# A mixture-of-experts step loop regrouped into two-step cycles, with its indirect DMAs in bursts

## What is computed

```python
# first half: x = x + layernorm(four S4D layers of layernorm(x))
z = _layernorm(x)                      # 8192 tokens x 128 channels
gating = z @ router_w.T                # 8 experts
probs = softmax(gating)
topk_weights, selected_experts = top_k(probs, 2)
for e in range(8):
    ew = sum(topk_weights * (selected_experts == e))
    h = z @ w1[e].T                    # 128 -> 512
    y = h[:, 256:] * silu(h[:, :256]) @ w2[e].T   # 256 -> 128
    out = out + y * ew
x = x + _layernorm(out)
```

## Time and profile before

| | us |
|---|---|
| median of the 3 runs (1073.33 to 1079.39) | 1076.9 |
| span of the profiled execution | 1076.0 |
| first silu of the expert loop starts | 700.9 |
| last second product starts | 1015.9 |
| PE, DVE, ACT, POOL busy, share of the span | 67%, 71%, 51%, 48% |

### The profile page before, as it was taken

How to read it: one execution, slowest core, us unless ns; L and a number is a source line. 1 busy time by engine, 2 the same in 40 slices (tenths; PEclk the granted TensorE clock), 3 DMA queues, 4 the chain that set the end, 5 groups by cost and what they waited for, 6 DMA issues and landing times.

```text
span 1076.0 us, 25371 instructions
## 1 busy us (share of the span) xinstructions
PE 724.1 (67%) x8523; PEld 611.2 (57%) x8524; DVE 761.7 (71%) x1889; ACT 551.7 (51%) x1197; POOL 521.3 (48%) x704
## 2 busy tenths in 40 slices
PE   0039267794879948795878876677877787787600
PEld 0028267673866658673876655565766676676500
DVE  8978867587675966588675998456555565565697
ACT  7628940188104941079103877333555574565645
POOL 2113224165432654257342766655676626536385
PEclk9999679797988979798988985578999999999955
DMA  7807699963999279982995002211343444444224
GB/s 283 349 1 223 210 385 386 331 243 122 358 340 380 74 258 385 329 299 65 359 386 227 1 11 79 68 36 52 108 125 122 124 120 119 124 117 121 86 82 151
DMA packets 120745, 205.48 MB, mean 191 GB/s; under 512 B 18381, under 2 KB 43481, under 8 KB 119769
## 3 DMA queue, kind: packets, MB, share of 16 engines
q1 hardware_dynamic: 112984, 188.66, 49.5%
q0 software_dynamic: 7680, 15.74, 5.4%
HBM read 167.40 MB, written 36.96 MB: 190 GB/s over the span
## 4 chain that ended last, share of the span: by engine, by line
issue 31%; PE 23%; POOL 20%; DVE 11%; ACT 8%; another core or an unknown queue 2%; DMA 2%; POOLq 1%; SPq 0%; ACTq 0%; DVEq 0%
PE bank L1197 10%; POOL zbuf L614 6%; POOL rstd_of L603 5%; PE bank L1216 4%; POOL toep L696 3%; PE bank L1032 3%; PE bank L1010 2%; ACT glu_work L969 2%; DVE glu_work L1797 1%; POOL sums L594 1%; DMA toep<-kernels_dram 1%; ACT toep L906 1%; ACT glu_work L949 1%; ACT ln_tmp L895 1%
## 5 line engine op out<-in xcount | busy, mean ns | idle before, releaser
L1032 PE MATMUL bank<-zbuf,toep 128*128 128x128 f16 (+3 forms) x3328 | 146.0, 206 | 90.1 <-DVE zbuf L1412 72.2
L1197 PE MATMUL bank<-toep 128*128 128x256 f16 x1248 | 162.2, 283 | 57.0 <-issue 31.0
L1032 PEld LDWEIGHTS bank<-zbuf,toep 128*128 128x128 f16 x3328 | 142.5, 102 | 94.2 <-issue 48.5
L1197 PEld LDWEIGHTS bank<-toep 128*128 (+1 forms) x1248 | 118.3, 101 | 90.5 <-issue 70.2
L614 POOL TENSOR_TENSOR zbuf<-zbuf,w_cur 128x256 f32<-128x256 f32 x120 | 89.7, 749 | 143.0 <-DVE zbuf L1476 142.9
L680 POOL DMA_INDIRECT z_sorted<-toep x120 | 124.2, 1035 | 68.3 <-remote 25.3
L1476 DVE TENSOR_REDUCE zbuf<-bank 128x256 f32<-128x512 f32 x128 | 87.1, 688 | 71.3 <-PE bank L1032 71.2
L1067 PE MATMUL bank<-wo_cur,glu_work 128*128 128x256 f32 x512 | 134.2, 407 | 2.5 <-ACT glu_work L840 2.2
L840 ACT ACTIVATE glu_work<-bank,unscale_cur 128x512 f32<-128x512 f32 x64 | 42.8, 668 | 167.4 <-PE bank L1054 167.3
L1067 PEld LDWEIGHTS bank<-wo_cur,glu_work 128*128 128x128 f32 x512 | 96.3, 198 | 43.4 <-issue 17.8
L1767 DVE SCALAR_TENSOR_TENSOR toep<-bank,toep 128x256 f16<-128x256 f32 x88 | 37.3, 424 | 93.5 <-issue 74.8
(11 more groups left out here) (269 smaller groups left out, 1488.8 us busy)
## 6 DMA issues: line engine op xcount, KB each, us to landing
toep<-kernels_dram SPq DMA_DIRECT2D x104, 1024.0 KB, 14.0
glu_work<-kernels_dram SPq DMA_DIRECT2D x16, 1024.0 KB, 14.1
toep<-z_sorted SPq DMA_DIRECT2D x88, 128.0 KB
y_sorted<-toep SPq DMA_DIRECT2D x88, 128.0 KB
z_sorted<-ln_tmp SPq DMA_DIRECT2D x3, 3072.0 KB, 23.8
toep_last<-kernels_dram SPq DMA_DIRECT2D x8, 1024.0 KB, 14.1
hres<-in_x SPq DMA_DIRECT2D x1, 4096.0 KB, 13.0
toep<-in_x SPq DMA_DIRECT2D x1, 4096.0 KB, 23.9
```

The source lines that it names most:

```text
L1032: last = MM(dst[:, d * (B // 4):, :], toep_slot(g)[:, c, d * P:(d + 1) * P, k], z_conv[:, 0:QUADS - d * (B // 4), g * GROUP + c].rearrange ...
L1197: last = MM(out[:, piece % 2 * XP:(piece % 2 + 1) * XP], w1_row[:, pw, bass.ds(e + piece * P, P)], xT_s[:, px * XP:(px + 1) * XP], start=( ...
```

## The change

It reorders the expert loop and changes how the tokens are divided. Nothing in the S4D layers changes.

- Three quads are dense (3, 14 and 15) instead of one, and three lists are sorted (12, 20 and 20 tiles; 19 + 27 + 27 = 73 blocks) instead of four. That makes 73 + 48 = 121 steps instead of 104, and 104 scatters and 104 gathers instead of 120 and 120.
- The sorted steps come first, the dense ones last.
- The loop goes in cycles of two steps. In a cycle PE transposes the two blocks of two cycles ahead, does both second products of two cycles back, then both first products. ACT does both silus, one copy of double width (512) for the two inputs, both high halves, and one copy of double width for the two outputs. DVE goes likewise.
- POOL waits once per burst, for `s_hid` of both steps of a cycle, and then issues 4 (both lists' scatters), 3 (gathers of lists 0 and 1) or 2 (list 2) indirect DMAs.
- The input and output blocks keep four slots each, `xT` has four instead of two; SP stores 12 blocks behind the load instead of 7.
- The last `count` and `places`, which stood in the loop, and `leads` with its exponentials move ahead of the loop. The dense steps, which PE ran in a hardware loop, are written out; only sorted steps 8 to 67 are in one.
- At the end, five gathered pieces (12, 16, 4, 12, 8 tiles) come first and the three dense quads last.

```diff
-CHOICES = ((0, 12), (12, 20), (32, 16), (48, 16))
+CHOICES = ((0, 12), (12, 24), (36, 20), (56, 8))
-DENSE = (3,)
+DENSE = (3, 14, 15)
-SEGMENTS = ((0, 12), (16, 16), (32, 16), (48, 16))
+SEGMENTS = ((0, 12), (16, 20), (36, 20))
+    CHOOSE_AT.append(max([_q + 10] + PLACE_AT[-1:]))
+    PLACE_AT.append(CHOOSE_AT[-1] + 2)
-GATHERED = [(0, 12), (16, 16), (32, 16), (48, 8), (56, 4), (60, 2), (62, 2)]
-PIECES = [(4 * q, 4) for q in DENSE] + GATHERED
+GATHERED = [(0, 12), (16, 16), (32, 4), (36, 12), (48, 8)]
+PIECES = GATHERED + [(4 * q, 4) for q in DENSE]
+EARLY = 4
+LOOPED = 8
+TURNS = (EXPERT_TILES - 6 - LOOPED) // UNROLL + 1
+STEPS = EXPERT_TILES + DENSE_STEPS
+LATE = 4
+BURSTS = (4, 4, 3, 2)
+def cycles(eng, cycle):
+    for s in range(-EARLY, LOOPED, 2):
+        cycle(Step(s))
     with eng.Fori(0, TURNS) as i:
+        for s in range(LOOPED, LOOPED + UNROLL, 2):
+            cycle(Step(s, i))
+    for s in range(LAST_STEPS, STEPS + LATE, 2):
+        cycle(Step(s))
...
+            LAG = 12
+            for n in range(0, EXPERT_TILES + LAG + 1, 2):
+                for tile in (n, n + 1):
+                    if tile < EXPERT_TILES:
+                        load(tile)
+                for tile in (n - LAG, n - LAG + 1):
+                    if 0 <= tile < EXPERT_TILES:
+                        store(tile)
...
+            def in_burst(size, most):
+                if left[0] == 0:
+                    burst[0] += 1
+                    pool.wait_ge(s_hid, min(2 * burst[0], most))
+                    left[0] = size
+                left[0] -= 1
...
-                    in_step()
+                    if transfers[0] >= 36:
+                        in_burst(BURSTS[0] if g == 1 else BURSTS[1], (FIRSTS[g] - 6) // 2 * 2 + 2)
+                    elif transfers[0] % 3 == 0:
+                        pool.wait_ge(s_z2T, min(6 + transfers[0] // 3, QUADS))
+                    transfers[0] += 1
...
+                    burst[0] = max(burst[0], (FIRSTS[g] + XTS[g]) // 2 + 3)
...
+                        in_burst(BURSTS[3] if g == SEGS - 1 else BURSTS[2], STEPS)
...
+            def cycle(s):
+                steps = two(s, lambda t: t.is_step)
+                for t in steps:
+                    silu(t)
+                ahead = two(s + EARLY, lambda t: t.is_sorted)
+                if ahead:
+                    xT_high(ahead)
+                if steps and s.at >= LATE:
+                    act.wait_ge(s_yps, (s + (len(steps) - LATE)).n)
+                for t in steps:
+                    inner_high(t)
+                done = two(s + -LATE, lambda t: t.is_sorted)
+                if done:
+                    act.wait_ge(s_yps, (s + (2 - LATE)).n)
+                    y_out(done)
...
+            def cycle(s):
+                if s.is_sorted:
+                    pe.wait_ge(s_xTsb, s.pair + 1)
+                for t in two(s + EARLY, lambda t: t.is_sorted):
+                    transpose_in(t)
+                for t in two(s + -LATE, lambda t: t.is_step):
+                    second_product(t)
+                for t in two(s, lambda t: t.is_step):
+                    first_product(t)
...
             gates()
+            leads()
+            def cycle(s):
+                steps = two(s, lambda t: t.is_step)
+                for t in steps:
+                    gated(t)
+                ahead = two(s + EARLY, lambda t: t.is_sorted)
+                if ahead:
+                    xT_low(ahead)
+                for t in steps:
+                    inner_low(t)
+                for t in two(s + -LATE, lambda t: t.dense):
+                    accumulate(t)
```

More of the change, by code:

```diff
@@ L711, in _ @@
                 scatter(g)
-            for i in range(len(DENSE), len(PIECES)):
+            for i in range(len(GATHERED)):
                 if PIECES[i][0] == SEGMENTS[-1][0]:
@@ L1135, in _ @@
                     route(q - 10)
[L1136 to L1138 removed]
+                    for c in range(SEGS):
+                        if q == max(CHOOSE_AT[c] + 1, 14):
                             count(c)
@@ L1225, in _ @@
+            cycles(pe, cycle)
         @block.vector
@@ L1801, in _ @@
-            tile_steps(dve, step, False)
+            def cycle(s):
[9 more added lines that the diff above has]
+                    accumulate(t)
+            cycles(dve, cycle)
```

310 lines of the change are left out of this document (130 added, 180 removed).

## The result

The changed kernel takes 1082.3 us (median of 20 runs, 1077.7 to 1087.3) against 1079.3 for the kernel before in the same runs: ratio 1.003, 95% interval 1.002 to 1.005. I had forecast 1063 us, so the time is 19 us above the forecast, and the change gains nothing here: the kernel is 0.3% slower.

What follows compares the result with a forecast made beforehand. Waits hold the loop: POOL's DMAs cost PE 0.93 us a step. Terms: 702.2 + 105.4 + 2.6 + 7.6 + 101.2 + 4.4 + 76 + 2.0 + 4.5 + 56.5 = 1062.4 us, median 1063, range 1045 to 1086.

Steps and rivals of the forecast that it cites:

- Rows of three beside sorted cycles: Loop's gathers of lists 0 and 1: 22 bursts of 4.6 us each, 101.2 us, bounds 4.4 to 4.7 each.
- a cycle takes the longer of PE's work and POOL's period: Expert loop: PE's 4.4 us sorted or 3.96 dense against POOL's period per burst; the longer sets the cycle.
- 1.3 us after `s_hid`: Loop: next first product needs only silu 0.60 and gate product 0.69; PE has 0.4 + 1.5 us to do first.
- the free cycle: Loop, between the gather lists: one cycle without a burst, 4.4 us.
- Rows of four and block 19: Loop's scatters: 17 bursts of 6.2 us, 105.4 us; waiting for block 19's load makes one cycle 13.8, 7.6 us lost.
- The start: Ahead of the loop: first two hidden products end at 702.2 us, bounds 4 us either way.
- may cost 2 us or nothing: Routing stretch before 690: the `count` of 20 tiles stands two quads later, costing 2 us or nothing.
- The dense part: Loop's bursts of two: PE bounds, 19 cycles of 4.0 us, 76 us, bounds 3.8 to 4.4 each.
- the rival of late instructions: Written-out PE code: instructions arrive late, 2 us at each of 10 transfers, 1083 us; chance 0.16.
- The rival of the port: Loop bursts: DVE stretches POOL's DMAs to 1.3 us each, 1102 us; chance 0.05.
- The end: Behind the last hidden product: drain 4.5 us, then DVE's pieces to the end 56.5 us, bounds 53 to 59.

Runs made afterwards that it cites:

- two_edits: Changed kernel with eight more of list 1's scatters ahead of the loop and PE's sorted cycles written out: 1062.5 us, 0.990 of before.
- free group: Experiments run on one chip with the kernel before beside them, where that kernel takes 988 to 993 us.
- before_no_pool: Kernel before without its scatters from the 37th on and all but the first gather of each piece: 994.1 us, 0.927 of before.
- eight_more_before_loop: Changed kernel with eight more of list 1's scatters issued ahead of the loop without a wait for PE's steps: 1071.0 us, 0.991 of before.
- held: Said of groups of runs in which the kernel before takes 1075 to 1081 us; the runs of the result were such.
- no_pool_again: Changed kernel without the last 68 scatters and all but the first gather of each piece, second run: 1029.5 us, 0.954 of before.
- changed_once_more: Changed kernel, unaltered, as a control: 1041.1 us, 1.051 of before.
- group 3: Four experiments: before without transfers, before with rows of four, one row of 28, and two edits; before took 1075.1 us.
- group 4: Four experiments: PE written out again, the experts' register load moved again, and two kernels with rows of three; before took 989.3 us.
- row_of_28: Changed kernel with list 1's last 28 scatters in one row instead of seven rows of four: 1086.8 us, 1.011 of before.
- three_edits: Changed kernel with PE written out, counting behind the last quad's transposes and eight more scatters ahead of the loop: 1085.2 us, 1.004 of before.

## Why the prediction was wrong, step by step

**Rows of three beside sorted cycles (the largest term, +9.2 us).** The step that failed is "a cycle takes the longer of PE's work and POOL's period", with 4.6 us from a single interval of before, and under it the reason given: the first product needs only silu and gate product "1.3 us after `s_hid`". PE's own 4.40 us stands: two_edits shows it where POOL rests (transposes at 853.81 and 858.21). The same kernel shows what three transfers do to it, and the changed kernel shows one such cycle whole. First two_edits, then the changed kernel:

```profile
853.81 0.60 PE L1184 MATMUL bank<-ident,toep 128*128 128x128 f32 x4
...
858.21 0.60 PE L1184 MATMUL bank<-ident,toep 128*128 128x128 f32 x4
...
878.92 0.94 POOL L711 DMA_INDIRECT zbuf<-y_sorted,toep  x1 [1.17 <-PE bank L1212]
...
883.20 1.44 PE L1230 MATMUL bank<-toep,glu_work 128*128 x23 [0.40 <-issue]
...
883.74 0.94 POOL L711 DMA_INDIRECT zbuf<-y_sorted,toep  x1 [1.03 <-PE bank L1212]
...
884.83 2.79 PE L1212 MATMUL bank<-toep 128*128 128x256 f16 x24 [0.18 <-issue]
```

```profile
878.01 2.79 PE L1212 MATMUL bank<-toep 128*128 128x256 f16 x24 [0.22 <-issue]
...
881.48 1.08 ACT L958 ACTIVATE glu_work<-bank 128x512 f32<-128x512 f32 x2 [1.84 <-PE bank L1212]
...
882.20 1.29 DVE L1797 TENSOR_TENSOR glu_work<-bank,glu_work 128x512 f32<-128x512 f32 x2 [1.93 <-issue]
...
883.03 2.79 PE L1212 MATMUL bank<-toep 128*128 128x256 f16 x24 [0.24 <-issue]
886.70 0.65 PE L1184 MATMUL bank<-ident,toep 128*128 128x128 f32 x4 [0.87 <-issue]
```

In two_edits the rows came 4.82 us apart (878.92 to 883.74), and PE stopped for 0.17 to 0.40 us. The stop of 0.40 in the second product cost nothing by itself, for the first gate product was ready only at 884.69. The one ahead of the first products is marked "issue", but it is the wait for data, as beside rows of four. In the changed kernel the first products ended at 880.80 and both silus started only at 881.48, 1.00 us after the row before (880.49); the first gate product ended at 882.89 (0.69 us from 882.20), and the next first products started at 883.03, 0.14 us later. The cycle is 2.79 + 0.68 + 1.55 = 5.02 us. So the cycle is neither PE's 4.40 nor POOL's 4.6 but the sum along a closed chain: first products, a post that comes late beside the row, silu, gate product, first products. Unheld, this chain has 1.48 us to spare (above, free group). I had read the late post, and used it for POOL's period alone, not for ACT, which waits for the same semaphore.

Of the 9.2 us, 15 ordinary intervals between rows of three beside sorted cycles, 4.91 us in the mean for 4.6, make 4.7. Four beside the first dense cycles (4.72) make 0.5. Three long ones (5.44, 5.62 and 11.17 around the free cycle, for 9.0) make 4.0. At 883.03 above a turn of the loop follows: branch and register load stand behind the first products, and PE idled 0.87 us before the transposes. I had left that bubble at nothing. Before has a second product at that place, and its turns cost 0.13 us (cycles of 4.41 and 4.54 us by turns in before_no_pool).

**Rows of four and block 19 (+2.4).** 6.33 us (mean of 13) for 6.2, and 14.9 us (747.22 to 762.11) for 13.8; the first two rows came as one, unbroken, and took 13.9 us (708.05 to 721.96) for the 15.0 of the sum, which was luck. The wait was where I had put it, at the transposes of block 19:

```profile
755.44 0.69 PE L1184 MATMUL bank<-ident,toep 128*128 128x128 f32 x2 [10.39 <-DMA toep<-z_sorted]
```

Working out its price from POOL's last row was right; not asking what it would bring to start those scatters earlier was the omission, since POOL stood idle for 10.38 us just ahead of the loop. eight_more_before_loop did that and gained 10 us.

**The start (+5.8).** 3.5 us of it are no part of the change. PE's routing begins at 612.95 in the changed kernel's profiled execution and at 609.45 in that of before, in work that is the same in both, and over all profiled executions it began anywhere from 608 to 618 us:

```profile
612.95 0.28 PE L1132 MATMUL bank<-router_sb,toep 128*128 128x8 f32 x2
...
691.30 1.88 PE L1132 MATMUL bank<-router_sb,toep 128*128 128x8 f32 x8 [2.36 <-ACT toep L933]
```

Of the other 2.3 us, 2.05 lie between the first routing and the last (78.35 us here, 76.30 before), and they are again a late post. I had said of the counting, which now stands ahead of the last transposes, that it "may cost 2 us or nothing". It moved the transposes by 0.1 us (74.61 us after the first routing, 74.52 before). But the copy that waits for them started 1.22 us after their end, behind a row of POOL's that ended at 688.60, and in the kernel before 0.04 us after it. First the changed kernel, then before:

```profile
687.56 1.38 PE L1120 MATMUL bank<-ident,toep 128*128 128x128 f32 x4
690.16 0.60 ACT L929 ACTIVATE toep<-bank 128x512 f16<-128x512 f32 x1 [5.80 <-PE bank L1120]
```

```profile
683.97 1.09 PE L1090 MATMUL bank<-ident,toep 128*128 128x128 f32 x4
...
685.10 0.60 ACT L918 ACTIVATE toep<-bank 128x512 f32<-128x512 f32 x1 [1.38 <-issue]
```

Whether the post would have come in time without the counting ahead of it is not shown: that edit alone ran only in a free group.

**What held.** The dense part: PE's first products 3.98 and 4.09 us apart by turns beside rows of two (4.0 forecast), steps 72 to 120 in 98.4 us held and 96.6 free.

```profile
961.96 2.80 PE L1212 MATMUL bank<-toep 128*128 128x256 f16 x24
962.19 1.27 POOL L711 DMA_INDIRECT toep<-y_sorted,toep  x1 [0.30 <-issue]
965.94 2.80 PE L1212 MATMUL bank<-toep 128*128 128x256 f16 x24
```

This is written-out code at PE's full rate, so the rival of late instructions is refuted there; PE written out from end to end needed 75 transfers on q8 for 61 and was no slower (1.051 of before in either form, in free groups). The rule of the Trainium skill, "Runtime: NRT & Kernel Launch", section on instruction fetch mechanics, that sequential prefetch is mostly hidden, fits the trace: no stop in dense cycles. Its other half, that a branch can force a fetch, does not explain the 0.87 us at the turn above: from 757 to 890 us the changed kernel shows no instruction transfer on q8. The rival of the port had 0.3 us of truth: the second transfer of a dense row takes 1.27 us for 0.95. The rule of the Trainium skill, "SBUF — State Buffer", section on the two separate sides, that DVE in a two-port mode keeps GpSimd from writing descriptors, would allow for that, but no run here shows that DVE is the cause. DVE's pace with and without transfers is the same (dense cycles 3.97 and 4.09 in no_pool_again and in changed_once_more). The end was right to 0.6 us: 60.4 us from the last silu on, for 61.0.

**Behind the sum.** I had seen that the loop would take about as long for 17 more steps, and so staked the whole gain of 13.6 us on the end and on periods known to 0.2 us, 60 times over. An error of 0.3 us in a cycle is 18 us. The gain of the forecast was no larger than that error, and a single interval of three transfers was no ground for the term: it is the first behind 17 us in which POOL stood idle.

## What to carry to other kernels

Where an engine is slowed by another's transfers, price a cycle by the number beside it, each length from a mean of many cycles (here, held: none, 4.4 sorted and 4.0 dense; two, 4.0 dense; three, 4.9 sorted; four, 6.3). If a post comes late, follow it to every engine that waits for it and add up the chain that it closes, instead of taking the larger of two engines' own times. Before moving work ahead of a pacing wait, ask how long a row grows when that wait is fulfilled early. And relief from a disturbance that is paid for with steps of work turns into a loss where the disturbance is absent: in free groups the changed kernel is 5.1% slower than before, 35 us by its own steps and 15 by the wait at block 19.

## What was unexpected of the hardware

The kernel before takes 8% less in some groups of runs than in others (988 to 993 us for 1075 to 1081), the changed one 4% (1041 for 1081). Clock (mean granted clock 0.86 to 0.89), transfer length (0.96 us) and the loads' landing times (13.9 us for 1 MB) are the same in both, and kernels without these transfers are within 0.4%. It isn't a matter of the chip alone, for group 3, held, and group 4, free, ran on the same one. What makes PE stop beside POOL's transfers in one and not in the other stays open.

In held groups PE's semaphores arrive 1.1 us after a row of four, 2.2 after one of 16 (before: row to 698.71, silu at 700.93), 3.5 after one of 23 and 4.2 after one of 28. What precedes the raster of 0.70 us is nearer to a count than to a time: from the row's start PE got 58 weight loads through in row_of_28 (5.7 us), 56 in the changed kernel beside its first eight transfers (5.8 us) and 69 in three_edits (12.7 us) before it slowed. These are three cases, and what is counted is open. In the loop it isn't the fetching of instructions: from 758 to 919 us row_of_28 shows none of the 16 KB transfers on the instruction queue q8, and PE stops there beside POOL's rows as elsewhere. For the long row itself that is not excluded: three such transfers lie between 705 and 760 us, one of them beside the row.
